# A fused decoder layer on one core: side work spread more densely beside attention, z packed by pairs of batches, expert weights requested behind the last packing

## What is computed

```python
# attention with a latent of L = 72 channels, H = 16 heads
Wdkv = x @ latent_w + latent_b                      # keys and values of all heads
q = einsum('btc,hcl->bhtl', x, Wd_w) + Wd_b
scores = einsum('bhtl,bsl->bhts', q, Wdkv) / sqrt(16)
attn = softmax(where(causal, scores, -inf))
y = einsum('bhts,bsl->bhtl', attn, Wdkv)
z = transpose(y, (0, 2, 1, 3)).reshape(b, t, 16 * 72)
attention = z @ out_w + out_b

# recurrence over the context, both directions: A' = ew * A + ek * v ; B' = ew * B + ek
wkv = (Af + Ab + cur * v) / (Bf + Bb + cur)
recurrence = sigmoid(r) * wkv

# eight experts, two chosen per row
logits = x @ router_w.T
routing_weights, selected = sparsemixer_eval(logits, 0.01)
for e in range(8):
    h = silu(x @ w_gate[e].T) * (x @ w_up[e].T)
    out = out + dense_w[:, e:e + 1] * (h @ w_down[e].T)

x = x + attention(layernorm(x))
x = x + recurrence(layernorm(x), ctx, ctx)
x = x + experts(layernorm(x))
```

## Time and profile before

| | before |
|---|---|
| median of three runs | 714.23 us |
| profiled execution | 716.7 us |
| its span | 715.0 us |
| PE busy | 571.5 us, 80% of the span |
| DVE busy | 418.3 us, 59% |
| ACT busy | 370.6 us, 52% |
| POOL busy | 356.2 us, 50% |
| DMA | 75.93 MB, mean 106 GB/s |

### The profile page before, as it was taken

One profiled execution on the slowest core, in us unless ns is written; L12 is line 12 of the kernel. 1 busy time (PEld: TensorE's weight loads), 2 busy tenths in 40 slices (PEclk: granted clock), 3 DMA queues, 4 the chain that ended last, 5 costly groups with the idle time before them and its releaser, 6 DMA issues.

```text
span 715.0 us, 11474 instructions
## 1 busy us (share of the span) xinstructions
PE 571.5 (80%) x3775; PEld 497.4 (70%) x3775; DVE 418.3 (59%) x873; ACT 370.6 (52%) x1000; POOL 356.2 (50%) x415
## 2 busy tenths in 40 slices
PE   0898799898999888999853207575989999999990
PEld 0786677776778676886533104475989999999990
DVE  4335356366537656657574462277897777777750
ACT  4267255665666455644451101255657777777750
POOL 2334355326623855718653356021586566676653
PEclk9999799999999999999875556685999999999996
DMA  8016355553545254453112004353769988888620
GB/s 291 2 20 66 45 67 77 69 62 53 94 85 83 42 68 79 85 71 63 28 26 67 1 1 146 113 190 95 156 170 246 242 228 227 226 223 223 171 46 0
DMA packets 62159, 75.93 MB, mean 106 GB/s; under 512 B 12370, under 2 KB 51540, under 8 KB 61844
## 3 DMA queue, kind: packets, MB, share of 16 engines
q1 hardware_dynamic: 51498, 64.91, 40.0%
q0 software_dynamic: 9856, 10.28, 8.0%
q10 hardware_dynamic: 746, 0.02, 0.1%
HBM read 48.90 MB, written 10.40 MB: 83 GB/s over the span
## 4 chain that ended last, share of the span: by engine, by line
PE 26%; DMA 25%; issue 14%; DVE 12%; POOL 11%; ACT 6%; SPq 4%; POOLq 1%; ACTq 0%; DVEq 0%
DMA out<-Y,TK 15%; PE P L766 6%; PE PO L871 6%; DMA zP<-ZT 5%; PE P L840 4%; PE P L858 4%; SPq L700 3%; POOL out L1649 3%; POOL xs L1625 3%; DMA qT<-qP 2%; ACT EB L1061 2%; PE P L848 2%; DVE ZT L1297 1%; DMA small<-ob 1%; POOL EB L1585 1%
## 5 line engine op out<-in xcount | busy, mean ns | idle before, releaser
L766 PE MATMUL P<-GT,WF 128*128 128x256 f32 x1104 | 145.3, 289 | 3.8 <-DVE GT L1210 3.8
L1061 ACT ACTIVATE EB<-P,small 128x128 f32<-128x128 f32 x256 | 90.4, 365 | 108.6 <-DVE small L1288 108.6
L1585 POOL TENSOR_TENSOR EB<-EB,small 128x512 f32<-128x512 f32 x64 | 77.3, 1208 | 136.7 <-DVE small L1292 136.5
L766 PEld LDWEIGHTS P<-GT,WF 128*128 128x128 f32 x1104 | 138.9, 196 | 4.0 <-DVE GT L1210 4.0
L1649 POOL DMA_INDIRECT out<-Y,TK x46 | 88.3, 1920 | 54.8 <-DMA out<-Y,TK 41.1
L1297 DVE COPY ZT<-P 72x512 f32<-72x512 f32 x64 | 43.3, 677 | 81.4 <-PE P L858 53.4
L858 PE MATMUL P<-PT,V 128*72 128x512 f32 x128 | 71.8, 645 | 12.1 <-DVE ZT L1297 8.6
L871 PE MATMUL PO<-Ow,zP 128*128 128x256 f32 x288 | 80.5, 416 | 0.0
L840 PEld LDWEIGHTS P<-KT,qT 72*128 72x128 f32 x512 | 69.6, 199 | 13.9 <-DMA qT<-qP 8.6
L840 PE MATMUL P<-KT,qT 72*128 72x128 f32 x512 | 71.1, 283 | 8.6 <-DMA qT<-qP 6.7
L766 PE MATMUL PO<-WF,HR 128*128 128x256 f32 x552 | 73.4, 292 | 2.6 <-issue 2.6
(11 more groups left out here) (180 smaller groups left out, 977.5 us busy)
## 6 DMA issues: line engine op xcount, KB each, us to landing
arena<-wf SPq DMA_DIRECT2D x36, 512.0 KB
WR<-wf SPq DMA_DIRECT2D x33, 512.0 KB
zP<-ZT SPq DMA_DIRECT2D x256, 36.0 KB
qT<-qP SPq DMA_DIRECT2D x63, 128.0 KB
X<-x SPq DMA_DIRECT2D x4, 512.0 KB, 12.0
cxa<-ctxin SPq DMA_DIRECT2D x4, 512.0 KB
out<-X SPq DMA_DIRECT2D x3, 512.0 KB, 4.4
xd<-XN SPq DMA_DIRECT2D x3, 512.0 KB, 3.3
```

The source lines that it names most:

```text
L766: r = e.matmul(o, lt(a), rt_(b), start=start and n == 0, stop=stop and n == 2, skip_group_check=skip)
L1061: e.activation(EB[i][:, j, :], S[:, 128 * j:128 * j + 128], ACT.Exp, bias=NM[i][:, j:j + 1], accum_out=SM[i][:, j:j + 1]).then_inc(s_exp, 1)
L1585: e.tensor_tensor(EB[i][:, :, :], EB[i][:, :, :], SM[i].unsqueeze(2).broadcast_to([128, 4, 128]), ALU.mult).then_inc(s_prob, 1)
```

## The change

- SHARE goes from 0.45 to 0.7 and PACE from 1.0 to 0.6. Side steps are handed out with more credit per turn and shorter pauses.
- For the first five pairs of batches the units of a pair alternate between its two batches. `ZT` and `zP` hold two batches side by side (`ZT` two buffers, `zP` two instead of three), and SP packs both with four DMAs of 1 KB pieces. Pairs six to eight go as before, unit by unit. Out-projections of the first ten batches move with it.
- `finish` moves from turn 63 to turn 66 (the turns are 0 to 67); the loads of token lists and weights of tiles 0 and 1 and the first splits are emitted there.
- The load into `WR` of odd tiles waits for the last scores where it waited for the last out-projection; the first two splits of tile 0 wait for the last queries where they waited for the last out-projection.

```diff
-SHARE, SHARE_TILES = 0.45, 4.0
+SHARE, SHARE_TILES = 0.7, 4.0
...
-PACE, PACE_TILES = 1.0, 0.1
+PACE, PACE_TILES = 0.6, 0.1
...
-UNITS = [(b // NB, b, hq) for b in range(B) for hq in range(4)]
...
+PAIRED = 5
+UNITS = ([(k, NB * k + i, hq) for k in range(PAIRED) for hq in range(4) for i in range(NB)]
+         + [(k, NB * k + i, hq) for k in range(PAIRED, NK) for i in range(NB) for hq in range(4)])
...
+def packing(n):
...
+    return (n // NB, NB) if n < PER * PAIRED else (4 * PAIRED + n - PER * PAIRED, 1)
...
+def packed_upto(b):
...
+    return 1 + max(packing(n)[0] for n, u in enumerate(UNITS) if u[1] == b)
...
-              [(24, stage_e(0, 0, GB)), (40, stage_e(1, 0, GB)),
-               (56, stage_e(2, 0, GB)), (56, plan(0)), (62, stage_e(3, 0, 2))],
+              [(26, stage_e(0, 0, GB)), (42, stage_e(1, 0, GB)),
+               (54, stage_e(2, 0, GB)), (54, plan(0)), (62, stage_e(3, 0, 2))],
...
+        at = 1 + max(n for n, u in enumerate(UNITS) if u[1] in ((b,) if b >= NB * PAIRED else (b - b % 2, b - b % 2 + 1)))
...
-            o_steps.setdefault(4 * b + (8 + i if b < 12 else 8 + i // 2 if b < B - 1 else 7), []).append((b, i))
+            if b >= NB * PAIRED:
+                at_i = at + (4 + i // 2 if b < B - 1 else 3)
+            else:
+                fast = 2 if b // NB == PAIRED - 1 else 1
+                at_i = at + 4 + (i // fast if b % 2 == 0 else 4 // fast + (i // 2 if b % 4 == 3 else i // fast))
+            o_steps.setdefault(at_i, []).append((b, i))
...
-    waiting, loaded = [], [False]
+    waiting = []
...
+    def split_w(j, k):
+        if j < NT:
+            emit("sw", j, k)
+            load_w(j + 2, k)
...
-        if n == NU:
+        if n == NU + 2:
+            finish(n, lambda: 0 in planned and NG - 1 in w_done)
+            for j in range(3):
+                emit("ltk", j)
+            for k in range(3):
+                load_w(0, k)
+            for k in range(3):
+                load_w(1, k)
...
-        if n == NU - 1 or (n > 58 and 0 in planned and not loaded[0]):
-            finish(n, lambda: 0 in planned and NG - 1 in w_done)
-            if not loaded[0]:
-                loaded[0] = True
-                for j in range(3):
-                    emit("ltk", j)
-                for k in range(3):
-                    load_w(0, k)
+            split_w(0, 0)
+            split_w(0, 1)
+            emit("tg", 0)
...
-    def split_w(j, k):
-        if j < NT:
-            emit("sw", j, k)
-            load_w(j + 2, k)
...
-    for k in range(3):
-        load_w(1, k)
-    split_w(0, 0)
-    split_w(0, 1)
-    emit("tg", 0)
...
-        ZT = [sb(f"ZT{i}", [L, 4, 128], fp32, s1) for i in range(2)]
-        zP = [sb(f"zP{i}", [128, NQ, 128], fp32, s1) for i in range(3)]
+        ZT = [sb(f"ZT{i}", [L, 4, 128 * NB], fp32, s1) for i in range(2)]
+        zP = [sb(f"zP{i}", [128, NQ, 128 * NB], fp32, s1) for i in range(2)]
...
-                _, b, hq = UNITS[n]
-                sp.wait_ge(s_z, n + 1)
-                if b > 2:
-                    sp.wait_ge(s_O, 4 * (b - 2))
-                for j in range(4):
-                    o = 8 * (4 * hq + j)
-                    e.dma_start(zP[b % 3][o:o + 8, :, :], ZT[n % 2][:, j, :]).then_inc(s_zd[n % 2], 16)
+                k, b, hq = UNITS[n]
+                z, nb = packing(n)
+                if nb == 1 or b % NB == NB - 1:
+                    sp.wait_ge(s_z, n + 1)
+                    sp.wait_ge(s_O, 4 * NB * (k - 1))
+                    c = slice(0, 128 * NB) if nb == NB else slice(128 * (b % NB), 128 * (b % NB) + 128)
+                    for j in range(4):
+                        o = 8 * (4 * hq + j)
+                        e.dma_start(zP[k % 2][o:o + 8, :, c], ZT[z % 2][:, j, c]).then_inc(s_zd[z % 2], 16)
...
-                    sp.wait_ge(s_O, 4 * B)
+                    sp.wait_ge(s_S, NU)
...
-                        pe.wait_ge(s_zd[j], 64 * (2 * b + 2))
+                        pe.wait_ge(s_zd[j], 64 * ((packed_upto(b) + 1 - j) // 2))
...
-                    p = e.matmul(o, zP[b % 3][:, m, :], Ow[:, m, :], start=False, stop=m == NQ - 1)
+                    p = e.matmul(o, zP[b // NB % 2][:, m, 128 * (b % NB):128 * (b % NB) + 128], Ow[:, m, :], start=False, stop=m == NQ - 1)
...
-                if j < 2:
+                if j == 0 and k < 2:
+                    ac.wait_ge(s_q, total["q"])
+                elif j < 2:
...
+                z, nb = packing(n)
+                c = 128 * (UNITS[n][1] % NB)
...
-                ve_.wait_ge(s_zd[n % 2], 64 * (n // 2))
-                e.tensor_copy(ZT[n % 2][:, :, :], YB[0:L, :].rearrange("p (h t) -> p h t", h=4)).then_inc(s_z, 1)
+                ve_.wait_ge(s_zd[z % 2], 64 * (z // 2))
+                e.tensor_copy(ZT[z % 2][:, :, c:c + 128], YB[0:L, :].rearrange("p (h t) -> p h t", h=4)).then_inc(s_z, 1)
...
```

## The result

| | before | after |
|---|---|---|
| median beside each other (20 runs each) | 713.57 us | 717.08 us |
| profiled execution | 716.7 us | 719.0 us |
| its span | 715.0 us | 717.2 us |
| last scores start | 364.15 us | 420.34 us |
| last scores to first expert matmul | 98.8 us | 46.0 us |

The ratio after to before is 1.0048, 95% interval 1.0024 to 1.0071: the changed kernel is half a per cent slower. 662 us was forecast, with 643 to 681 as the range. The 52.8 us that the tail gave came back, and 57 us went into the loop of units.

What follows compares the result with a forecast made beforehand. PE was taken to bound attention and the later experts, a latency chain the stretch between. Tail -56.8, moved work +5, density +5, pairs -5 and first tiles 0 summed to -51.8, giving a 662 us median, range 643 to 681.

Steps and rivals of the forecast that it cites:

- The bound and the tail: Loop: PE the bound; last scores to first expert matmul: a latency chain, 98.8 us becoming 42, a gain of 56.8.
- Work moved into the loop: Attention loop: PE's side work from the stretch of 66.4 us moves in, about +5 us at 2.4 GHz.
- "I take +5" for density: Attention loop: cost of denser side work on in-order DVE, +5 us, ends -3 and +25.
- The sign named for it: Loop term would be wrong if the last scores started after 380 or before 358 us.
- If PE's idle time grows as DVE's share: Attention loop: with DVE rising from 59% to 71%, PE's idle time goes from 19.6 to 24 us.
- so a transpose may wait for its ACT copy: Attention loop: pauses shortened to 0.6 may make PE's transposes wait; counted within the +5 us for density.
- The upper end of +25: Attention loop: about 0.8 us more for each of 32 DVE scans, if all met POOL work.
- theory B: Loop, from the experiments, not the prediction: DVE is too full for its in-order work; no chance given.
- A: Loop, from the experiments: short pauses make PE stop for normalised rows, then run at slow clock; no chance given.
- Rival 4: Loop: DVE delays row maxima, PE stops and loses its fast clock; 70 to 80 us more, about 735; chance 0.03.
- Pairs: Attention loop: packing z by pairs, 256 issues becoming 176, cuts PE waits; -5 us, ends 0 and -12.
- First tiles: Experts' first 70 us: same work, half group only started earlier; 0 us, ends -8 and +6.

Runs made afterwards that it cites:

- e8: The changed kernel with credit 0.45 and pauses 1.0, both as before, the rest of the change kept; 722.06 us, ratio 1.014.
- e1: The changed kernel with pauses restored to 1.0, credit still 0.7; 697.49 us, ratio 0.9716.
- e7: The changed kernel with credit 0.55 and pauses 1.0; 717.1 us, ratio 1.0048.
- e10: The changed kernel with pauses 1.0 and the recurrence's DVE scans and reciprocals cut to an eighth, the rest uncomputed; 681.49 us, one run.
- e3: The changed kernel with z packed batch by batch instead of by pairs; 724.31 us, ratio 1.011.
- e11: The changed kernel with credit 0.45, pauses 1.0 and z packed batch by batch; 723.37 us, one run.
- e12: The changed kernel with PACE 1.0, shorter pauses in recurrence and routing, and a longer one ahead of LN3's transposes; 692.6 us, ratio 0.9696.
- e5: The changed kernel with the recurrence's DVE scans and reciprocals cut to an eighth, the rest uncomputed; 700.97 us, one run.
- e4: The kernel before with only credit 0.7 and pauses 0.6; 740.6 us, ratio 1.0352.

## Why the prediction was wrong

- **The bound and the tail: right.** -56.8 us forecast, -52.8 measured (46.0 for 42). The wait of some 15 us for gathered rows and batch 15 mostly at 1.2 GHz are in the rows above. That PE would be the bound of the loop was right too, and is why each stop counted in full.
- **Work moved into the loop: right.** "On PE it is 13.5 us less some 3 of attention, at half clock: about +5": 4 to 5 estimated from the rows, +-3.
- **"I take +5" for density: the step that failed.** The sign named for it came true: the last scores start at 420.3, behind 380. Credit and pauses measured +51.8 (24.1 from e8 to e1, 27.7 from e1 to after), of which 4 to 5 are the moved work: some +47. The other 5.2 us of the loop are what e8 has over before. Two things were wrong in it. The first is the formula "If PE's idle time grows as DVE's share": idle grew from 28.5 to 63.4 us while DVE's busy time in the loop rose by a sixth. DVE's share did not even rise to the 71% forecast: from unit 9 on it is 188.8 of 333.1 us, 57% for 59%, because the loop stretched. In the rows followed above, DVE, in order, delays PE by what stands ahead of one short instruction, not by its mean load. Between 0.45 and 0.7 of credit each us of DVE work added cost 0.9 of the loop (e7, e8, e1), and taking it out gave 0.4 back per us (e10). The second is the clause "so a transpose may wait for its ACT copy": the mechanism was named and got a part of 5 us. The pauses were worth 28 (e1), the XN stops being their main part.
- **The working had the means.** A unit is five turns and took 5.2 us, so a turn is about one microsecond. The pause for the inverse root went from 5 turns to 3, and those between the shift and the transposes from 2 and 4 to 1 and 2. Fourteen steps of 279 ns are 3.9 us, longer than the 3 turns, before any scan slows them; the chain had no room left. The upper end of +25, from scans that meet POOL, was about the size of theory B's 24 us, but that is luck, and it left A out: of the 32 scans in after's loop six took more than 1.4 us, and their excess over 1.21 us is 7.4 us in all (before: four of 24, 2.5 us).
- **The clock.** Rival 4 (0.03) had half of the mechanism: stops of some microseconds, each with slow work behind it. Its cause, row maxima delayed by DVE, is not what PE stood for in after's rows, where XN, the queries and z lead. It was two thirds as large as its case: 17 us of clock and 35 of idle time, where the case had 70 to 80. (That case does not add up: by the rule that gives 52 us for a fifth, a third at 1.2 GHz costs 87 us before any stop.) The bound set for it, a clock below 0.85 in the loop, was too far: 0.90 sufficed, since idle time cost twice as much as the clock.
- **Pairs: -5 forecast.** In the dense kernel -3.8 in the loop (e3), in the sparse one +2.2 (e11, one run); both lie within the scatter of single executions. The rule of the Trainium skill, "DMA: Bandwidth & Descriptors" (why small descriptors are slow), that moves within SBUF do not pay for small descriptors, is not tested by this, since half of the issues go too. DVE's wait for z fell from 21.7 to 1.1 us in the loop, further than forecast, and gave little. Unit 8 takes 12.0 us at a clock of 0.72 for 15.1 at 0.63, but the eight units ahead of it took 47.6 us for 42.0.
- **First tiles: 0 forecast, -1.2 measured** (250.9 for 252.1). That was luck of these numbers: at PACE 1.0 all of the experts take 257 to 269 us (e12 to e10) for 250.9, because work that finishes just before the experts in one plan falls into them in another.

Not settled: how much of the 24 us by credit is DVE itself and how much is POOL slowed beside DVE (e10 takes DVE's work out and POOL's busy time falls by 22.6 us as well; scans slowed by POOL are only some us of it), and what makes PE wait for the copy of the queries in the dense loop (9.1 us, 4.8 in e1, 3.3 in e5, 0.5 in e10), which no run here changes by itself.

## What to carry to other kernels

When side work is packed closer into an in-order pipeline, cost it by the latency of each chain against the place of its consumer on the bound engine, not by mean shares: a pause shorter than the chain ahead of it can become a stop of the bound engine, and the slow clock behind a stop is charged on top. Shorten pauses only where the consumer is off the bound engine, and check what the plan leaves for the next stage: here 52.8 us gained in the tail were lost in the loop; the old pauses of e1 kept some 17 to 20 us of them and the mixed pauses of e12 22, figures that the runs do not tell apart.

## What the runs showed of the hardware

- A stop of 4.7 us of PE was followed by 9.7 us at a clock of 0.53, and then by 1.00; after a stop of 3.6 us (at 221.22) the next 9.8 us had 0.83. Before, only one stop in the loop was that long, the 4.5 us of the earlier trace rows; after has seven.
- DVE and POOL slow each other both ways, and by more than the length of one instruction: small POOL steps of 0.20 us took 1.05 to 1.16 beside scans, and one scan of usually 1.2 us took 4.32 beside three POOL operations of 1.05 to 1.18, ending 1.1 us behind the last of them. With light scans POOL's busy time in the loop fell from 183.0 to 160.4 us at the same 249 instructions. The exclusive lock of the Trainium skill, "SBUF — State Buffer" (the two separate sides), agrees with the first pair: the steps of 1.05 and 1.16 us are those that start beside a scan of 1.2.
- A scatter issued by POOL takes longer beside DVE's scans: 4.45 us in after and 3.92 and 4.26 in e4, each with three scans back to back beside it, 1.90 and 1.92 before, with a scan of 1.2 beside its start, and 0.96 as the median of 32. With scans of an eighth of the length (e5) none of the 32 took more than 1.27.
